# Batched bilinear products on one Trainium2 core: a bound of two tiles on the stores that are open

## The reference

```python
bilinear = jnp.einsum('bie,ied->bid', feature, weight)    # each field times its own 64x64 matrix
out = jnp.einsum('bid,bjd->bij', bilinear, feature)       # 200x200 scores of each sample
```

## Time and profile before

| | us |
|---|---|
| median of 3 runs | 311.1 |
| the three runs | 307.51 to 311.19 |
| profiled execution, its time | 306.8 |
| its span, first to last instruction | 305.0 |
| TensorE busy, of the span | 243.2 (80%) |
| VectorE / ScalarE busy | 152.8 / 130.1 |
| bytes moved by DMA | 112.35 MB, 368 GB/s over the span |

### The profile page before, as it was taken

One profiled execution on the slowest core, in us unless ns is written; L12 is line 12 of the kernel. 1 busy time (PEld: TensorE's weight loads), 2 busy tenths in 40 slices (PEclk: granted clock), 3 DMA queues, 4 the chain that ended last, 5 costly groups with the idle time before them and its releaser, 6 DMA issues.

```text
span 305.0 us, 14640 instructions
## 1 busy us (share of the span) xinstructions
PE 243.2 (80%) x6800; PEld 210.9 (69%) x6800; DVE 152.8 (50%) x180; ACT 130.1 (43%) x181; POOL 12.5 (4%) x23
## 2 busy tenths in 40 slices
PE   6839849999877586999867785898985774998990
PEld 2437749888776476878866675866885674996970
DVE  0153634556755443537644454634765554775621
ACT  2153515445544324245444243542653451665420
POOL 2004800000000000000000000000000000000000
PEclk9996997999999979899999799999999999999997
DMA  7999997999999999968999999986999999599995
GB/s 219 415 417 357 363 410 302 324 376 373 369 360 416 407 419 420 409 280 354 374 366 408 383 411 417 388 355 248 389 371 391 408 387 417 210 402 381 409 408 218
DMA packets 22172, 112.35 MB, mean 368 GB/s; under 512 B 4320, under 2 KB 4320, under 8 KB 21856
## 3 DMA queue, kind: packets, MB, share of 16 engines
q1 hardware_dynamic: 22112, 111.43, 92.6%
HBM read 29.49 MB, written 81.92 MB: 365 GB/s over the span
## 4 chain that ended last, share of the span: by engine, by line
PE 76%; issue 16%; DMA 2%; SPq 2%; DVE 1%; ACT 1%
PE psum L322 50%; PE psum L285 17%; PE psum L339 8%; DMA w_sb<-w_dram 2%; SPq L166 2%; PE psum L305 1%; DVE tile L355 1%; ACT mixed L376 0%; ACT w_sb L390 0%; SPq L178 0%
## 5 line engine op out<-in xcount | busy, mean ns | idle before, releaser
L322 PE MATMUL psum<-x_sb,mixed 64*64 64x200 f32 x3072 | 163.1, 351 | 14.0 <-issue 12.5
L322 PEld LDWEIGHTS psum<-x_sb,mixed 64*64 64x64 f32 x3072 | 133.3, 139 | 27.9 <-issue 17.9
L355 DVE COPY tile<-psum 128x800 f32<-128x800 f32 x100 | 99.2, 992 | 88.6 <-PE psum L322 79.8
L355 ACT COPY tile<-psum 128x800 f32<-128x800 f32 x100 | 82.4, 826 | 70.2 <-PE psum L322 54.0
L285 PE MATMUL psum<-x_sb,w_sb 64*64 64x64 f32 x3072 | 64.4, 221 | 35.1 <-issue 34.2
L285 PEld LDWEIGHTS psum<-x_sb,w_sb 64*64 64x64 f32 x3072 | 61.7, 134 | 40.5 <-issue 37.7
L376 ACT COPY mixed<-psum 64x512 f32<-64x512 f32 x48 | 27.8, 580 | 43.2 <-PE psum L285 42.6
L376 DVE COPY mixed<-psum 64x512 f32<-64x512 f32 x48 | 33.1, 689 | 16.7 <-PE psum L285 15.5
L378 ACT COPY mixed<-psum 128x512 f32<-128x512 f32 x24 | 14.1, 586 | 36.3 <-PE psum L285 36.2
L378 DVE COPY mixed<-psum 128x512 f32<-128x512 f32 x24 | 16.6, 691 | 22.3 <-PE psum L285 22.2
L339 PE MATMUL psum<-x_sb,tails 128*32 128x200 f32 x512 | 25.0, 342 | 0.1
(11 more groups left out here) (5 smaller groups left out, 1.7 us busy)
## 6 DMA issues: line engine op xcount, KB each, us to landing
out_dram<-tile SPq DMA_DIRECT2D x192, 400.0 KB, 5.6
x_sb<-x_dram SPq DMA_DIRECT2D x64, 400.0 KB, 6.9
out_tail_dram<-tile SPq DMA_DIRECT2D x8, 400.0 KB, 4.2
w_sb<-w_dram SPq DMA_DIRECT2D x1, 1152.0 KB, 15.2
w_sb<-w_dram SPq DMA_DIRECT2D x4, 256.0 KB, 7.3
w_sb<-w_dram SPq DMA_DIRECT2D x1, 1024.0 KB, 13.1
```

Source lines behind the costliest of these rows:

```text
L322: last = nc.tensor.matmul(psum[half_rows(pair), n % BANK_PAIRS * 2 + h, a * FIELDS:(a + 1) * FIELDS], mixed[half_rows(h), (CHUNKS * g + c) ...
L355: copy(tile[:, k % SLOTS, engine], psum[:, bank:bank + 2, 0:2 * FIELDS]).then_inc(copied[engine], 1)
```

## The change

SP gets one more wait. Before the stores of tile k (from k = 2 on) it waits until both stores of tile k - 2 have landed. So the stores of two tiles at most are open at a time. The wait stands in front of the wait for the copies of tile k, and so also behind the load that follows tile k - 1. Nothing else differs: same tiles, same slots, same order on every engine, same DMAs.

```diff
+OPEN_TILES = 2
...
             for k, (kind, g, *rest) in enumerate(OUT_TILES):
                 to = out_tail[g] if kind == "tail" else out[g, rest[0], rest[1]]
+                if k >= OPEN_TILES:
+
+                    old = k - OPEN_TILES
+                    sp.wait_ge(slot_out[old % SLOTS], STRIP_STORES * (old // SLOTS + 1))
                 for e in range(2):
                     n = NUMBER[("tail", g, e) if kind == "tail" else ("score", g, *rest, e)]
                     sp.wait_ge(copied[e], COPIES[n][e])
```

## The result

The changed kernel takes 321.0 us (median of 4 runs, 317.95 to 325.57) where the kernel before takes 310.6 (4 runs). The ratio is 1.0325, with a 95% interval of 1.021 to 1.044: it is slower. The forecast was 309.5 us and no change that can be told; the measured time lies close to the figure of the slower rival, 322. TensorE's clock is not the cause: one of the four runs had a mean granted clock of 0.961, as the profiled execution of before had, and took 319.04 us against its 306.8.

The account below looks back on a forecast made before the run. TensorE, waiting for code queued behind stores, and the DMA engines were taken to bound the kernel by turns. Terms -13.6 - 1.8 + 12.4 + 1.4 = -1.6 us gave 305.2 us, 309.5 on the runs' scale; range 298 to 322.

Parts of the forecast that it names:

- slower rival: Stores without loads, chiefly from 245 us on: the round trip sets 2.45 us a tile; +10.8 us, 322 us; chance 0.22.
- last rival: TensorE's code comes no sooner: its 43.1 us of waits stay, no stock; +3.4 us, 314.5 us; chance 0.10.
- Gain 1: Mainly stretches of stores alone: code comes sooner, TensorE builds a stock, DMA idle time goes; 13.6 us gained.
- Loss 1: The 55 tiles without a load: the wait's round trip makes the pace 2.225 us a tile; 12.4 us lost.
- Loss 2: The 45 tiles with a load: engines that finish first idle at times, 0.03 us a tile; 1.4 us lost.
- Gain 2: The kernel's end: the last store lands sooner with only one other tile in front; 1.8 us gained.
- A: Theory after the result: a code packet delays one DMA engine, the others run dry; e13 at 1.02 to 1.04.

Follow-up runs that it names:

- e3: The kernel before with most of TensorE's matmuls left out, all copies, loads and stores kept, no bound on open tiles; 285.4 us.
- e8: The changed kernel with the bound of two tiles only before the 45 tiles that have a load behind them; 1.011 times the kernel before.
- e4: e3 with the bound of two open tiles added; 298.8 us.
- e16: e4 with TensorE's work from 245 us on cut again, to one matmul a score unit; 294.8 us in one run.
- e13: The changed kernel with single waits: three stores open at most, each store waiting for the one three in front; 1.105 times the kernel before.

## Why the prediction was wrong, point by point

**What bounds the kernel, right; why code is late, not shown.** Two regimes that take turns, and slots that hardly matter as long as TensorE sets the pace: e3, without TensorE's bound, is 7% faster and its DMA engines idle for 0.4 us. The waits for code fell from 43.1 to 23.8 us (about 20 was forecast) when fewer bytes stood in front. The last rival had them stay, so it is out as a forecast. That the fewer bytes in front brought the code sooner is not shown, though: TensorE was also held back by its slots, for 16.4 us, and while it stands a code packet has time to come. In e3 stores take as long to land as before (a median of 5.8 us against 5.6), and no matmul waits for code, in a kernel with 16 packets whose TensorE waits for copies instead. So the runs don't decide on the rule by which each DMA engine takes turns between queues packet by packet (the Trainium skill, "DMA: Bandwidth & Descriptors", section "Queues, rings and completion order").

**Gain 1, the step that failed first.** It was priced at 13.6 us, all of the DMA engines' idle time that TensorE had caused, because TensorE would have a stock. It got the stock: SP was up to 13 us behind the copies, and copies waited 45.3 us for slots. But idle time of one cause was traded for idle time of another. Over the whole kernel it went up by 6.6 us. e8 shows what the stock brings where no bound follows it: from 28 us on TensorE's waits for code fell from 43.1 to 31.2 us, yet the 52 steps from one tile's landing to the next in the stretches without loads took 116.4 us where they had taken 119.2, a gain of 2.8.

**Loss 1, mis-sized.** The pace of 2.225 us was the mean of a tile that meets a code packet (2.45) and one that does not (2.0). The second is right: 1.9 to 1.97 us measured. The first holds for one tile, but both open tiles wait for the late engine, and the next two are issued late by as much. So a packet costs the whole stream 1.0 us or more, not the 0.45 us that the sum charged for it. The same 52 steps took 127.8 us in the changed kernel, 2.46 each. Against 2.0 that is a loss of 24 us, with 24 code packets among them, where the sum had 12.4; the slower rival's 24.8 us at a pace of 2.45 comes near it, though not for its reason. It took the latency for a plain round trip; the changed kernel, e4 and e16 show 3.8 to 4.1 us for tiles with no packet in the way.

The 24 us count gain 1 as come in full. Counted from e8, where gain 1 was 2.8 us, the bound costs 11.4 us in these steps, about what was forecast. No run tells the two ways of counting apart. By either the two terms come to 8.6 us lost in these steps where the sum had 1.2 us gained, and this is the greater part of the miss.

**Loss 2, mis-sized.** Taken at 1.4 us, with a bound of 4.5. e8 puts it at 1.1% (0.1 to 2.2%), some 3.4 us, and in its trace it is not idle time, as was assumed, but 4.6 us of slower packets.

**Gain 2, right in sign.** 1.8 us forecast, 3.0 measured in the two profiled executions as the fall of SP's last wait from 5.6 to 2.6 us.

**The estimate from the Trainium skill.** The page "DMA: Bandwidth & Descriptors", section "Anatomy of one DMA — SWDGE (gpsimd) path", gives 2.0 us plus bytes over 436 GB/s for a DMA of GpSimd, and from it came an estimate of 3.9 us a tile, and so a loss of nothing. The undisturbed tiles agree, at 3.8 us for two DMAs of SyncE. It is still not the answer, since the tiles that set the pace are the disturbed ones.

What stays open: why e13 lost three times what A had it lose, what makes a burst of slow packets, and how much sooner code alone is worth. How much of what a code packet costs is its own transfer and how much slower packets beside it was not measured either. No run varied the code packets alone: e4 and e16 have fewer of them because TensorE has less work, and the two attempts to bring them back failed.

## What to carry to other kernels

Size a bound on open transfers by what is left in the queue at the moment a wait ends, and not only by what is open at most: it must cover the round trip and the worst delay of any one engine. Here three stores of 1 us left did and two did not, and the same number of open bytes cost 3.3% in pairs and nothing when waited for singly. The number open at most counts as well: with two left, three at most lost 10.5%. Take the latency that counts from the latest of the engines and from all transfers that are open with it, and before pricing idle time as a gain ask which idle time takes its place.

## What the runs showed of the hardware that was not expected

- A code packet of 16.4 KB on the code queue goes with one of the 16 DMA engines being late by 1.9 us (a tile of 5.7 us instead of 3.8), more than the 0.9 us that the packet itself takes in the trace.
- The same bytes take the DMA engines a different busy time: 255.8 us without a bound, 261.5 with one (e3, e4), and 275.7 in e13 against 262.4 in the kernel before, in bursts of packets that take over 0.4 us in place of 0.244.
- Waits for code can vanish under a full queue of stores: e3's stores take a median of 5.8 us to land, as before, and none of its matmuls waits for code where TensorE waits for copies (16 packets).
- Short matmuls of 8 columns, put in as filler, brought TensorE's mean granted clock to 0.588, from 0.775 in e3 without them, and the kernel to 459 us.
